# Attention scores by blocks of 128 keys on two 64x128 tiles of the array, in place of 64 keys on four 64x64 tiles

## The reference

```python
qf, kf = features(q), features(k)          # B, 16 heads, 256 tokens, 64 features (2 nodes x 32), all positive
kv_cur = cumsum(kf[..., :, None] * v[..., None, :], tokens)     # over this token and all earlier ones
k_cur  = cumsum(kf, tokens)
ctx = einsum('bhtf,bhtfd->bhtd', qf, kv_cur)
den = maximum(einsum('bhtf,bhtf->bht', qf, k_cur), 1e-6)
out = x + (ctx / den) @ Wout + bout + experts(xn)
```

## Time and profile before

| what | value |
|---|---|
| median of 3 runs | 442.91 us (442.89 to 442.96) |
| the profiled execution | 442.89 us, of which the span of its instructions is 441.1 us |
| granted TensorE clock, mean | 0.998 of full |
| PE matmul busy | 431.3 us, 98% of the span, 5726 matmuls |
| PE weight load busy | 361.3 us, 82% |
| VectorE, ScalarE, GpSimd busy | 354.1 (80%), 317.0 (72%), 186.5 us (42%) |
| matmuls of `scores` (line 1144) | 2 x 1024 |

### The profile page before, as it was taken

How to read it: one execution, slowest core, us unless ns; L and a number is a source line. 1 busy time by engine, 2 the same in 40 slices (tenths; PEclk the granted TensorE clock), 3 DMA queues, 4 the chain that set the end, 5 groups by cost and what they waited for, 6 DMA issues and landing times.

```text
span 441.1 us, 15832 instructions
## 1 busy us (share of the span) xinstructions
PE 431.3 (98%) x5726; PEld 361.3 (82%) x5726; DVE 354.1 (80%) x887; ACT 317.0 (72%) x534; POOL 186.5 (42%) x278
## 2 busy tenths in 40 slices
PE   7899999999999999999999999999999999999996
PEld 4578888888888888888888988888898888888885
DVE  7898878979788797978979797897978789686663
ACT  4767695858768586785868768585876858577691
POOL 5424444543435444343643443454344445434320
PEclk9999999999999999999999999999999999999999
DMA  4400221030202003020110302002020200302001
GB/s 96 105 25 7 58 48 28 2 63 14 52 22 47 18 6 59 12 48 24 27 33 12 59 12 48 24 7 52 12 57 15 48 12 0 61 1 56 7 2 25
DMA packets 45323, 14.37 MB, mean 33 GB/s; under 512 B 35376, under 2 KB 45168, under 8 KB 45296
## 3 DMA queue, kind: packets, MB, share of 16 engines
q1 hardware_dynamic: 44448, 13.48, 14.8%
q10 hardware_dynamic: 720, 0.53, 0.4%
q0 software_dynamic: 128, 0.01, 0.1%
HBM read 3.44 MB, written 2.10 MB: 13 GB/s over the span
## 4 chain that ended last, share of the span: by engine, by line
PE 96%; DVE 2%; issue 1%; ACT 1%; POOL 0%; DVEq 0%; POOLq 0%
PE p_s L1144 10%; PE x L1094 9%; PE p_t L1144 8%; PE x L1300 7%; PE x L1262 7%; PE x L1309 6%; PE x L1321 6%; PE x L1157 5%; PE p_s L1157 5%; PE x L1286 4%; PE x L1235 4%; PE x L1290 3%; PE x L1287 3%; PE p_s L1129 2%; PE x L1246 2%; PE p_s L1330 2%
## 5 line engine op out<-in xcount | busy, mean ns | idle before, releaser
L488 POOL TENSOR_TENSOR s_sb<-s_sb,causal 128x256 f32<-128x256 f32 x96 | 68.2, 732 | 76.6 <-ACT s_sb L584 76.6
L578 ACT ACTIVATE feat<-arg,f_bias 128x1024 f32<-128x1024 f32 x64 | 71.8, 1147 | 8.9 <-DVE arg L857 8.7
L1144 PEld LDWEIGHTS p_s<-feat 64*64 64x64 f32 x1024 | 38.8, 132 | 15.8 <-issue 14.1
L329 POOL TENSOR_TENSOR qk_sq<-qkv 128x512 f32<-128x512 f32 x15 | 15.6, 1041 | 83.3 <-DVE qkv L834 83.3
L1144 PE MATMUL p_s<-feat 64*64 64x256 f32 (+3 forms) x1024 | 49.5, 309 | 0.0
L857 DVE TENSOR_SCALAR arg<-p_s,f_low,f_high 128x1024 f32<-128x1024 f32 x32 | 42.9, 1340 | 7.4 <-PE p_s L1129 4.6
L482 POOL TENSOR_TENSOR s_sb<-s_sb,causal 128x512 f32<-128x512 f32 x30 | 37.6, 1274 | 25.3 <-ACT s_sb L590 25.3
L1144 PE MATMUL p_t<-feat 64*64 64x256 f32 (+3 forms) x1024 | 47.1, 299 | 0.1
L857 DVE TENSOR_SCALAR arg<-p_t,f_low,f_high 128x1024 f32<-128x1024 f32 x32 | 42.7, 1336 | 0.0
L1144 PEld LDWEIGHTS p_t<-feat 64*64 64x64 f32 x1024 | 41.3, 133 | 1.7 <-issue 0.3
L606 ACT ACTIVATE disp<-x 128x512 f32<-128x512 f32 x32 | 17.4, 594 | 26.6 <-PE x L1246 26.6
(11 more groups left out here) (167 smaller groups left out, 1055.3 us busy)
## 6 DMA issues: line engine op xcount, KB each, us to landing
xin<-in_L_attn_x_dram SPq DMA_DIRECT2D x31, 64.0 KB, 2.3
out_dram<-out_sb SPq DMA_DIRECT2D x31, 64.0 KB, 2.1
se_rows<-n_L_ffn_slot_embeds_dram SPq DMA_DIRECT2D x2, 128.0 KB, 4.2
w_f<-in_L_ffn_w_dram SPq DMA_DIRECT2D x1, 256.0 KB, 4.1
w_sb<-in_L_ffn_w_dram SPq DMA_DIRECT2D x1, 256.0 KB, 3.9
stack_t<-stack SPq DMA_TRANSPOSE x16, 4.3
wqkv_f<-in_L_attn_Wqkv_dram ACTq DMA_DIRECT2D x1, 192.0 KB, 3.9
bqkv_bc<-in_L_attn_bqkv_dram ACTq DMA_DIRECT2D x1, 192.0 KB, 5.0
```

What stands on the lines that cost most here:

```text
L488: pool.tensor_tensor(v, v, m, ALU.mult).then_inc(mb_ok, 1)
L578: nc.scalar.activation(feat[:, k:k + 2, :], arg[:, k:k + 2, :], ACT.Exp, bias=f_bias[:, 0:1]).then_inc(fe_ok, 1)
L1144: mm = nc.tensor.matmul(dst[rows:rows + 64, u, o:o + hi - lo], f[:, T + keys:T + keys + 64], f[:, lo:hi], start=True, stop=True, skip_grou ...
```

## The change

The table `BLOCKS` has two key groups of 128 in place of four of 64. The first covers all 256 queries, the second queries 128 to 255. A matmul has 64 rows and 128 columns now, and writes all 128 partitions. The lower left quarter of each diagonal square, which held stale values times a zero of the mask, holds scores of later keys times the same zero.

```diff
-BLOCKS = ((0, 0, 0, T, 0), (64, 64, 64, T, 64), (128, 0, 128, 192, 256), (192, 64, 128, T, 256))
+BLOCKS = ((0, 0, T, 0), (128, 128, T, 256))
...
                 dst = (p_s, p_t)[p % 2]
-                for keys, rows, lo, hi, o in BLOCKS:
+                for keys, lo, hi, o in BLOCKS:
                     for u, done in enumerate((sa_ok, sb_ok)):
                         f = feat[64 * u:64 * u + 64, p % 4, :]
-                        mm = nc.tensor.matmul(dst[rows:rows + 64, u, o:o + hi - lo], f[:, T + keys:T + keys + 64],
+                        mm = nc.tensor.matmul(dst[:, u, o:o + hi - lo], f[:, T + keys:T + keys + 128],
                                               f[:, lo:hi], start=True, stop=True, skip_group_check=True)
-                        if keys == 192:
+                        if keys == 128:
                             mm.then_inc(done, 1)
```

## The result

The changed kernel takes 457.94 us (median of 4 runs, 457.65 to 458.03) against 442.91 us before. The ratio is 1.0333, with a 95% interval of 1.0321 to 1.0345: 15.0 us slower, where 14.9 were forecast. The profiled execution took 457.65 us with a span of 455.6 us.

What follows compares the result with a forecast made beforehand. PE, start to start, bounds the kernel: pairs of 1.25 + 0.22 + 0.055 = 1.52 us add 15.7 us in 16 items, less 0.8 of waits, 14.9 on 442.9: 457.8 us. Range 454.4 to 464.8 us.

Steps and rivals of the forecast that it cites:

- The bound: Steady state on PE: time is what PE needs from start to start; a score pair goes to 1.52 us.
- Streaming: Score blocks on line 1144: each half streams 768 columns in place of 640, 0.22 us more per pair.
- The first load: Start of each score pair: the unhidden weight load covers 128 columns in place of 64, 0.055 us more per pair.
- The low end of my own range: Start of each pair: if the first weight load costs no more than before, -3.4 us, 454.4 us.
- The other loads: Weight loads behind a pair's first: 0.107 us each, hidden beside matmuls of at least 128 columns, so no cost.
- Change of tile shape: Edges between score pairs and neighbouring PE work: same number, still 0.09 us each, nothing gained or lost.
- The pair that waits: Pair at 208.16, 13 or 14 such: its 0.1 us wait for VectorE's clip of `p_t` goes, leaving 1.52 us.
- Rival (a): Start of a pair's second block: loads there, or of one more step, aren't hidden; 6.8 us, 464.7 us, chance 8%.
- The first item: PE's waits before both projections (up to 0.47 us) and for a third-pair clip (0.3) absorb growth: -0.8 us.
- rival (e): Across each item: PE waits hidden by the tails absorb the added 0.98 us; 442.9 us, chance 2%.
- Copies and masks: VectorE, ScalarE and GpSimd: same instructions on the same 384 columns, moving with the score blocks, no cost.

Runs made afterwards that it cites:

- the pair of runs: Kernel before, every quarter streaming 768 columns: 454.64 us; changed kernel, halves cut to 640 columns in steps of 128 or more: 445.52 us.
- the run with 64 columns: Changed kernel with the second key group cut to the last 64 queries, so each half streams 256 + 64 columns twice: 454.95 us, ratio 1.0282.

## Why the prediction was right

**The bound.** "PE from start to start" held: the 64 pairs grew by 15.3 us, and the first item's waits and its earlier start account, to 0.1 us, for what the span grew less (14.5).

**Streaming.** Taken as 0.22 us a pair, measured as 0.21 twice, on quarters (1.25 to 1.46) and on halves (1.30 to 1.51). The reasoning behind it, that quarters and halves all work at the same time and only the columns of one count, is shown by the pair of runs.

**The first load.** Taken as 0.055, measured as 0.05 twice (1.46 to 1.51 and 1.25 to 1.30). The first block came out at 0.75 us where 0.77 was forecast, so the clean pair at 1.51 and not 1.52. The low end of my own range, no growth, is out.

**The other loads.** Taken as hidden, and shown: 0.03 us for four more steps. But 128 columns (0.107 to 0.111 us) are hardly longer than the load of 128 columns (0.107); the run with 64 columns shows the cost at half that length, and nothing between was measured. The prediction put it as "exactly this fits" and was safe only because the changed kernel has no shorter matmul.

**Change of tile shape.** Same number, same 0.09: the edges in the timeline are unchanged.

**The pair that waits.** Right that the wait goes (1.36 to 1.51, not to 1.61). The working was wrong in size: it put the clip 0.26 us ahead of its turn and counted all of it as room, while the release (0.11) and the load (0.107) have to fit in as well. At most 0.03 us were left. Rival (a) was much nearer than its 8% and its text say: with 0.13 us more on VectorE it happens in these 14 pairs.

**The first item.** Half right. The rows of the changed kernel, PE and the clip on VectorE:

```profile
28.44 0.92 PE L1144 MATMUL p_s<-feat 64*128 64x256 f32 x8
...
33.04 1.16 PE L1300 MATMUL x<-w_sb,hid_t 128*128 128x128 f32 x8
34.36 0.38 PE L1129 MATMUL p_t<-stack_t,omega_st 64*128 64x512 f16 x2
...
39.12 1.34 DVE L857 TENSOR_SCALAR arg<-p_t,f_low,f_high 128x1024 f32<-128x1024 f32 x1
...
39.55 0.92 PE L1144 MATMUL p_s<-feat 64*128 64x256 f32 x8
...
41.42 0.50 PE L1094 MATMUL x<-se_hi,xt_hi 128*128 128x512 f32 x1
```

The third pair in the kernel before:

```profile
39.22 1.34 DVE L857 TENSOR_SCALAR arg<-p_t,f_low,f_high 128x1024 f32<-128x1024 f32 x1
...
39.74 0.77 PE L1144 MATMUL p_s<-feat 64*64 64x256 f32 x16
...
41.37 0.50 PE L1094 MATMUL x<-se_hi,xt_hi 128*128 128x512 f32 x1
```

The waits before the projections took up most of the two pairs' growth: line 1300's 8 steps start 0.29 us later than in the earlier trace rows, the second projection 0.18 us earlier, so 0.47 us are gone between them, all that the prediction allowed for. The wait for the clip in the third pair didn't take 0.3 us: the pair takes 1.87 us where I put 1.52, and 1.63 before, so it grew by 0.24, nearly as much as any other. Seen from the pair's start the clip ends 0.09 us later than before (0.91 in place of 0.82), so only 0.07 of the 0.16 us that the first block grew fell into the wait. From the clip's end to line 1094 0.96 us pass in place of 0.81, since all of the second block comes behind it. Why the clip came later, seen from PE, stays open. From the first of the three pairs to line 1094 12.98 us pass, 12.71 before: 0.27 us where three pairs of 0.27 less 0.8 left nothing in my sum. Against it stands the item's growth, measured as 0.94 and put at 0.98 (0.6 us in 16). From the first pair to the end of the span the kernel grew by 14.7 us where the sum had 14.9. That it came so close is in part luck, with these two errors against each other.

**Absorbed by other waits, rival (e).** Only the 0.1 us of the waiting pair and the first item's waits took anything up, 0.5 us of the latter and not 0.8. The copy put ahead of the clip shows that this pair is the place where PE waited: 0.13 us later there is 0.12 us longer in the pair.

**Copies and masks.** VectorE 353, ScalarE 316, GpSimd 187 us, within 1.2 us of before, and no new wait of PE for them.

## What to carry to other kernels

Where small tiles of the array ran at the same time, the price of a group of matmuls was the columns that one tile streams, the first load and the change of tile shape, as long as no step was shorter than the next load; count these per tile, not instructions. Smaller stationary blocks paid here because they let a part of the triangle be skipped, 640 columns in place of 768, and the larger tile saved nothing by halving the instruction count. A wait that is just hidden has to be measured at the load behind it, not at the matmul.

## What the runs showed of the hardware

A step was as long as the longer of its matmul and the next load: with 128-column f32 loads, matmuls of 64 columns had a mean duration of 244 ns, with 64-column loads 217, and a pair with such steps took 1.46 us where the same 640 columns in longer steps took 1.30. At 128 columns and more the loads behind the first cost next to nothing (0.03 us for four more steps in each half). The three changes between 64x128 and 64x64 in a pair cost 0.51 us together, which fits 0.09 us and an open load for each.
